# Rotary embedding of the first stage: from a rotation matmul on TensorE to a lane shuffle on VectorE, with a new order of work

## What is computed

```python
x = x + attn(layernorm(x))            # stage 0: the only one with the rotation
x = x + xattn(layernorm(x), ctx)      # stage 1
x = x + ffn(layernorm(x))             # stages 2 to 7, then a last layer norm

def _apply_rope(x, cos, sin):         # on queries and keys of stage 0, per head of 16 channels
    x1, x2 = (x[..., :8], x[..., 8:])
    return concatenate([x1 * cos - x2 * sin, x2 * cos + x1 * sin], axis=-1)
```

## Time and profile before

| | us |
|---|---|
| median of 3 runs | 5278.08 |
| lowest, highest | 5269.10, 5292.41 |
| the profiled execution: time | 5268.01 |
| the profiled execution: span | 5266.2 |
| PE busy in the span | 4823.1 |
| DVE busy | 3453.1 |
| ACT busy | 2479.3 |
| POOL busy | 707.9 |

### The profile page before, as it was taken

How to read it: one execution, slowest core, us unless ns; L and a number is a source line. 1 busy time by engine, 2 the same in 40 slices (tenths; PEclk the granted TensorE clock), 3 DMA queues, 4 the chain that set the end, 5 groups by cost and what they waited for, 6 DMA issues and landing times.

```text
span 5266.2 us, 149908 instructions
## 1 busy us (share of the span) xinstructions
PE 4823.1 (92%) x59612; PEld 3530.9 (67%) x59612; DVE 3453.1 (66%) x6058; ACT 2479.3 (47%) x4737; POOL 707.9 (13%) x1734
## 2 busy tenths in 40 slices
...
PEclk8999999999999999998999999999999999999999
...
DMA packets 42888, 44.64 MB, mean 8 GB/s; under 512 B 11552, under 2 KB 41888, under 8 KB 42144
## 3 DMA queue, kind: packets, MB, share of 16 engines
...
## 4 chain that ended last, share of the span: by engine, by line
issue 55%; PE 28%; DVE 7%; POOL 6%; ACT 1%; POOLq 1%; DVEq 0%; ACTq 0%
PE banks L945 27%; DVE row_max L909 3%; POOL neg_max L719 2%; POOL neg_max L722 2%; POOL x_tok L704 1%; POOL inv_std L698 1%; PE banks L1064 1%; DVE pair_sums L930 1%; ACT probs L818 1%; DVE rope_s L874 1%; DVE k_parts L887 0%; POOL var_eps L695 0%; PE banks L994 0%; DVE n_tok L930 0%; DVE x_tok L942 0%
## 5 line engine op out<-in xcount | busy, mean ns | idle before, releaser
L909 DVE TENSOR_REDUCE row_max<-banks 128x4 f32<-128x1024 f32 (+1 forms) x1280 | 1313.3, 1068 | 350.5 <-PE banks L945 348.0
L818 ACT ACTIVATE probs<-banks 128x1024 f32<-128x1024 f32 (+1 forms) x1280 | 1137.8, 935 | 487.6 <-PE banks L945 469.9
L945 PE MATMUL banks<-k_parts,q_parts 32*128 32x256 f32 (+1 forms) x15360 | 652.1, 306 | 166.8 <-DVE row_max L909 130.9
L945 PEld LDWEIGHTS banks<-k_parts,q_parts 32*128 32x128 f32 x15360 | 541.9, 201 | 333.7 <-DVE row_max L909 162.4
L930 DVE TENSOR_TENSOR pair_sums<-probs 128x512 f32<-128x512 f32 x512 | 368.1, 719 | 524.3 <-ACT probs L818 403.3
L945 PE MATMUL banks<-q_parts,k_parts 32*128 32x256 f32 (+1 forms) x13824 | 605.4, 304 | 75.1 <-DVE row_max L909 32.0
L945 PEld LDWEIGHTS banks<-q_parts,k_parts 32*128 32x128 f32 (+1 forms) x13824 | 470.6, 188 | 291.6 <-issue 163.4
L719 POOL TENSOR_TENSOR neg_max<-row_max,zeros 128x8 fp32r<-128x8 f32 x640 | 166.4, 260 | 3680.1 <-DVE row_max L909 3680.1
L945 PE MATMUL banks<-node_t,w_n 128*128 128x256 f32 x2560 | 633.2, 390 | 5.5 <-ACT node_t L835 5.5
L930 DVE TENSOR_TENSOR n_tok<-probs 128x512 f32<-128x512 f32 x512 | 364.2, 711 | 286.7 <-PE banks L945 167.9
L945 PEld LDWEIGHTS banks<-node_t,w_n 128*128 128x128 f32 x2560 | 461.4, 190 | 125.2 <-issue 46.1
...
## 6 DMA issues: line engine op xcount, KB each, us to landing
...
```

What stands on the lines that cost most here:

```text
L818: done(act.activation(probs[s][0:rows, g % 2, 2 * p:2 * p + 2, 0:kt, :] .rearrange("p c k t -> p c (k t)"), psum[0:rows, b0:b0 + 2, 0:kt * T],
L909: done(dve.reduce_max(row_max[s][:, g, 2 * p:2 * p + 2, :].rearrange("p c q -> p (c q)"), psum[:, b0:b0 + 2, :].rearrange("p c (q t) -> p ...
L945: return nc.tensor.matmul(bank_ap, lhs, rhs, start=start, stop=stop, **kw)
```

## The change

The matmul by rot is gone, for queries and keys (QR and KR, with their two banks). In its place DVE shuffles the lanes within each group of 32 partitions: lane p takes lane 16*(p//16) + (p+8)%16, which swaps the halves of each head. The sign goes into the sine table, once in the prologue: PE multiplies rot by a column of ones, and DVE multiplies the table by the resulting column. A copy of one element stands ahead of each shuffle. KI now waits for the shuffle of the queries and no longer for QR. The multiplication by the sines reads rope_s in SBUF, where it read a bank. And the whole ORDER is another one, with other banks; its new words are shown in parts.

```diff
+TURNED = [16 * (p // 16) + (p + 8) % 16 for p in range(ROWS)]
...
             elif k in ("QS", "KS"):
-                dve.wait_ge(sem["proj_ready"], reached(at, "proj_ready", (k[0] + "R", s, j)))
-
+                dve.wait_ge(sem["rope_in_kept"], reached(at, "rope_in_kept", (k[0] + "I", s, j)))
                 old = [("KH", 1 - s, j), ("KL", 1 - s, j)] if k == "QS" else [("QH", s, j, 1), ("QL", s, j, 1)]
                 dve.wait_ge(sem["high_kept"], reached(at, "high_kept", old[0]))
                 dve.wait_ge(sem["low_kept"], reached(at, "low_kept", old[1]))
-                done(dve.tensor_tensor(rope_s[:, :, :], both_of((k[0] + "R", s, j)),
+                dve.tensor_copy(rope_seen[:, :], rope_in[s][:, 0, 0:1])
+                done(dve.stream_shuffle(rope_s[:, :, :], halves(rope_in[s]), TURNED), "rope_turned", a)
+                dve.wait_ge(sem["rope_turned"], reached(at, "rope_turned", a))
+                done(dve.tensor_tensor(rope_s[:, :, :], rope_s[:, :, :],
                                        sin_t[:, :].unsqueeze(1).to_broadcast([P, KC, T]), ALU.mult), "rope_sin", a)
...
                 if k == "KI":
                     act.wait_ge(sem["rope_cos"], reached(at, "rope_cos", ("QC", s, j)))
-                    act.wait_ge(sem["proj_ready"], reached(at, "proj_ready", ("QR", s, j)))
+                    act.wait_ge(sem["rope_turned"], reached(at, "rope_turned", ("QS", s, j)))
...
-            elif k in ("QR", "KR"):
-                wait_for(pe, at, a, ("rope_in_kept", (k[0] + "I", s, j)))
-                done(matmul(bank_of(a), rot[:, :], rope_in[s][:, :, :].rearrange("p k t -> p (k t)"), True, True),
-                     "proj_ready", a)
...
+                pe.wait_ge(rest_loaded, 16 * len(rest_copies))
+                last = nc.tensor.matmul(psum[:, 0, NODES * KC:NODES * KC + 1], rot[:, :], all_ones[:, 0:1],
+                                        start=True, stop=True)
...
+                dve.tensor_scalar(sin_t[:, :], sin_t[:, :], psum[:, 0, NODES * KC:NODES * KC + 1], None,
+                                  ALU.mult).then_inc(chain_v, 1)
```

The order at the places that the prediction speaks of, old and new. The head of the table, that is the restart of the loop:

```diff
-KI0.1 LNP0.1 V1.0@5 LNN0.1 KS1.0 TR0.1@3 KH0.1 KL0.1 TRE0.1 KH1.0 KL1.0 Q0.1@6 QB0.1 QH0.1.0 QH0.1.1 QL0.1.1
-QL0.1.0 VE1.0 S1.0.0@0 SB1.0.0 MX1.0.0.0 MX1.0.0.1 S1.0.1@4 SB1.0.1 MX1.0.1.0 MX1.0.1.1 S1.0.2@0 SB1.0.2
+LOADX0 +LOADC0 LNP0.1 LNN0.1 VE1.0 KS1.0 KH0.1 TR0.1@0 TRE0.1 Q0.1@2 KL0.1 KH1.0 QB0.1 KL1.0 QH0.1.0 QH0.1.1
+QL0.1.1 S1.0.0@4 QL0.1.0 SB1.0.0 S1.0.1@0 MX1.0.0.0 SB1.0.1 MX1.0.1.1 MX1.0.0.1 MX1.0.1.0 S1.0.2@4 SB1.0.2
```

Stage 0 of slot 0, with the last stage of slot 1 (all words from the first projection to the first transposed scores):

```diff
-+Q0.0@2 +QB0.0 OB0.7.1 +QI0.0 FA0 S1.7.1@4 SB1.7.1
-MX1.7.1.0 +QR0.0@3 MT1.7.0@0 MR1.7.0 +QC0.0 +K0.0@2 +KI0.0 MX1.7.1.1 ST1.7.0@4 +QS0.0 +QH0.0.1 SX1.7.0 EX1.7.0.1
-EX1.7.0.0 NM1.7.1 MT1.7.1@0 MR1.7.1 LNS0.7 +QL0.0.1 +KR0.0@1 +KC0.0 +KS0.0 V1.7@2 VE1.7 +KH0.0 LNP0.7 ST1.7.1@4
-SX1.7.1 EX1.7.1.1 PV1.7.0@1 PA1.7.0.1 PA1.7.0.0 LNN0.7 PS1.7.0 RC1.7.0 +KL0.0 FG0 NR1.7.0 FX0 +V0.0@0 EX1.7.1.0
-+VE0.0 +S0.0.0@4 +SB0.0.0 +MX0.0.0.0 +MX0.0.0.1 +S0.0.1@0 +SB0.0.1 +MX0.0.1.0 +MX0.0.1.1 +NM0.0.1 PA1.7.1.1
-STORE0 +XB0.0 +LOADX1 OA1.7@5 +S0.0.2@0 +SB0.0.2 +MX0.0.2.1 +MX0.0.2.0 +NM0.0.0 PA1.7.1.0 PV1.7.1@4 +S0.0.3@0
-+SB0.0.3 +MX0.0.3.1 +MX0.0.3.0 OB1.7.0 +MT0.0.0@7 PS1.7.1 RC1.7.1 +MR0.0.0 +NM0.0.2 NR1.7.1 +NM0.0.3 +ST0.0.0@0
++Q0.0@5 MX1.7.0.0 +QB0.0 MX1.7.0.1 OB0.7.1 +QI0.0 FA0 S1.7.1@0 +QC0.0 SB1.7.1 NM1.7.0 MX1.7.1.0 MT1.7.0@5
+MR1.7.0 ST1.7.0@4 MX1.7.1.1 SX1.7.0 EX1.7.0.1 +QS0.0 +K0.0@3 EX1.7.0.0 V1.7@2 PA1.7.0.0 +KI0.0 NM1.7.1 PA1.7.0.1
++QH0.0.1 +KC0.0 +QL0.0.1 MT1.7.1@1 MR1.7.1 ST1.7.1@4 +KS0.0 VE1.7 SX1.7.1 EX1.7.1.1 PV1.7.0@1 PS1.7.0 LNS0.7
++KH0.0 LNP0.7 EX1.7.1.0 +KL0.0 RC1.7.0 PA1.7.1.0 +S0.0.0@4 +SB0.0.0 NR1.7.0 +V0.0@0 +MX0.0.0.0 +VE0.0 +MX0.0.0.1
+LNN0.7 +S0.0.1@4 +SB0.0.1 +NM0.0.0 FG0 +MX0.0.1.0 OA1.7@3 +MX0.0.1.1 +NM0.0.1 +S0.0.2@4 FX0 +SB0.0.2 STORE0
++MX0.0.2.0 PV1.7.1@1 +MX0.0.2.1 +XB0.0 PA1.7.1.1 +S0.0.3@4 +SB0.0.3 +MX0.0.3.1 +MT0.0.0@0 +LOADX1 +MR0.0.0
+PS1.7.1 RC1.7.1 OB1.7.0 +MX0.0.3.0 NR1.7.1 +ST0.0.0@4
```

The tail of the table, stage 0 of slot 1 ahead of the restart:

```diff
-+PV0.0.3 +PA0.0.3.1 +PA0.0.3.0 +PS0.0.3 +RC0.0.1 FX1 +QS1.0 STORE1 +NR0.0.1 +K1.0@1 +OB0.0.0@6 +OB0.0.1 +KI1.0
-+V0.1@1 +XA0.0 +LNS0.1 +VE0.1 +KC1.0 +QH1.0.1 +QL1.0.1 +KR1.0@6 +K0.1@2 +XB1.0
++QS1.0 +PS0.0.3 +XB1.0 +RC0.0.1 +OB0.0.0@0 +K1.0@2 +NR0.0.1 +OB0.0.1 +KI1.0 +V0.1@1 +QH1.0.1 +XA0.0 +KC1.0
++K0.1@6 +LNS0.1 +V1.0@3 +KI0.1 +VE0.1 +QL1.0.1
```

And two places in the later stages (the words of PE alone), transposed scores of stage 2 and of stage 4:

```diff
-V0.2@0 MT0.2.0@3 ST0.2.0@0
+MT0.2.0@7 V0.2@4 ST0.2.0@4
...
-MT0.4.1@3 S1.4.0@4 SB1.4.0 PV0.4.0@3 PS0.4.0 ST0.4.1@4
+S1.4.0@0 SB1.4.0 MT0.4.1@5 PV0.4.0@6 PS0.4.0 ST0.4.1@0
```

More of the change, by code:

```diff
@@ new lines @@
+MT0.1.1@2 ST1.0.2@4 PA1.0.1.0 SX1.0.2 EX1.0.2.1 PV1.0.1 PS1.0.1 EX1.0.2.0 PA1.0.2.1 MT0.1.0@1 RC1.0.0 PA1.0.2.0
+ST1.0.3@4 SX1.0.3 MR0.1.0 K1.1@3 EX1.0.3.0 PV1.0.2@1 EX1.0.3.1 PS1.0.2 MR0.1.1 PA1.0.3.0 ST0.1.0@4 SX0.1.0
+PA1.0.3.1 EX0.1.0.1 PV1.0.3 NR1.0.0 EX0.1.0.0 PS1.0.3 RC1.0.1 ST0.1.1@4 SX0.1.1 OB1.0.0@0 EX0.1.1.0 NR1.0.1
+V1.1@2 OB1.0.1 VE1.1 +LOADC1 KI1.1 XA1.0 PV0.1.0@1 EX0.1.1.1 PS0.1.0 LNS1.1 ST0.1.2@4 SX0.1.2 EX0.1.2.0 PV0.1.1
+LNP1.1 PS0.1.1 EX0.1.2.1 XB0.1 RC0.1.0 LNN1.1 ST0.1.3@4 SX0.1.3 EX0.1.3.0 NR0.1.0 TR1.1@3 EX0.1.3.1 PV0.1.2@2
@@ new lines @@
+SX1.1.2 K0.2@6 EX1.1.2.1 NR1.1.0 EX1.1.2.0 QH0.2.1 KH0.2 ST1.1.3@0 SX1.1.3 OB1.1.0@5 EX1.1.3.1 KL0.2 EX1.1.3.0
+QL0.2.1 PV1.1.2@4 QL0.2.0 S0.2.0@0 SB0.2.0 MX0.2.0.0 PS1.1.2 PV1.1.3 PS1.1.3 MX0.2.0.1 RC1.1.1 K0.3@6 NM0.2.0
+NR1.1.1 KH0.3 OB1.1.1 KL0.3 XA1.1 S0.2.1@0 SB0.2.1 LNS1.2 MT0.2.0@7 V0.2@4 MR0.2.0 MX0.2.1.1 LNP1.2 VE0.2
+MX0.2.1.0 ST0.2.0@4 LNN1.2 SX0.2.0 NM0.2.1 TR1.2@2 MT0.2.1@1 TRE1.2 MR0.2.1 K1.2@0 EX0.2.0.1 EX0.2.0.0 Q1.2@2
+KH1.2 PA0.2.0.0 QB1.2 PA0.2.0.1 QH1.2.0 PV0.2.0@3 KL1.2 QH1.2.1 PS0.2.0 QL1.2.0 RC0.2.0 S1.2.0@4 SB1.2.0
@@ new lines @@
+PS1.2.1 MX0.3.0.1 RC1.2.1 OB1.2.0 K1.4@1 NR1.2.1 MX0.3.0.0 OB1.2.1 KH1.4 NM0.3.0 NE1.2.0 S0.3.1@4 NE1.2.1
+SB0.3.1 MX0.3.1.0 MT0.3.0@0 Q1.3@3 MR0.3.0 QB1.3 MX0.3.1.1 V1.3@2 QH1.3.0 QH1.3.1 QL1.3.1 KL1.4 VE1.3 ST0.3.0@4
+QL1.3.0 SX0.3.0 NM0.3.1 S1.3.0@0 EX0.3.0.0 SB1.3.0 MX1.3.0.0 EX0.3.0.1 MX1.3.0.1 PV0.3.0@5 NM1.3.0 MT0.3.1@7
+PA0.3.0.1 MT1.3.0@4 MR0.3.1 ST0.3.1@0 PA0.3.0.0 SX0.3.1 EX0.3.1.0 PS0.3.0 K0.5@6 EX0.3.1.1 PA0.3.1.0 MR1.3.0
+PA0.3.1.1 RC0.3.0 S1.3.1@0 SB1.3.1 KH0.5 MX1.3.1.0 PV0.3.1@4 PS0.3.1 MX1.3.1.1 RC0.3.1 OA0.3@7 NR0.3.0 ST1.3.0@0
```

124 lines of the change are left out of this document (55 added, 69 removed).

## The result

The changed kernel takes 5462.3 us (median of 4 runs, 5437.8 to 5482.3), the kernel before on the same chip 5276.7: a ratio of 1.035, 95% interval 1.0315 to 1.0385. It is 3.5% slower. I had predicted 5244 us and a range of 5185 to 5325; the time lies outside the range, on the other side of "no change". Behind two of the later tables stand positions that I worked out from the traces: each step of the written order was found in the record of VectorE or ScalarE, its distance taken from LNN0.1, the first VectorE instruction of its turn, and the mean taken over the 15 turns of the loop.

A forecast was written before the change was run, and what follows sets the result against it. PE, 92% busy, looked like the bound, but DVE sets the pace during the row maxima. Terms +1.7 - 1.15 - 1.75 - 0.9 = -2.1 us a turn, times 16 is -34 us, giving 5244 us; range 5185 to 5325.

The forecast's parts named there:

- slot 0, QS0.0 to PA0.0.0.0: Slot 0's first stage: DVE is the limit and PE's saving is worth nothing; +1.7 us a turn.
- slot 1, up to the restart: Slot 1's first stage: PE loses 1.99 us, the query's 0.84 on DVE is charged in full; -1.15 us a turn.
- restart to MX1.0.0.0: Loop restart: value projection moved ahead, restart to slot 1's first scores falls from 7.70 to 5.96 us; -1.75 us a turn.
- the other stages: Remaining stages: new order mostly repeats the old with other bank numbers, two waits change; -0.9 us a turn, bounds +2 to -3.
- The shuffle's price: On DVE, each product costs one shuffle pass of 0.69 us and a one-element copy of 0.15, 0.84 us more.
- rival 4: On DVE, the shuffle takes 1.4 us or masks cost extra: 45 us more, 5289 us; chance 0.05.
- rival 2: Sine pass on DVE collides with POOL, up to 2.7 us a turn eat the gain: about 5278 us; chance 0.17.
- My bound of +2: Upper bound in us a turn for the other stages, for new waits that were not found.
- the 0.5 for the waits between query and key: Slot 0, ahead of the maxima: estimated us for waits for ScalarE that the new order puts between query and key.
- The group cycle: Slot 0's four score groups share one set of banks, so each takes a cycle of 3.44 us.
- 1.0 us comes back: Slot 0: keys' low parts no longer collide with POOL's gain and shift, 2.42 us for two instructions against 1.41.
- Rival 3: Clock falls each turn behind slot 0's maxima, costing 51 to 90 us: 5295 to 5334 us; chance 0.20.

The follow-up runs named there:

- e1: The changed kernel's shuffle and signed sines in the old order of work with its old banks, against the kernel before; 5305.2 us, ratio 1.0069.
- e10: e5 with slot 0's keys and their copy back in the old sequence, from the previous turn's last maxima to slot 0's value projection; 5409.5 us, ratio 1.0259.
- e8: e1 without copy and shuffle, so no engine does the rotation and VectorE multiplies unrotated queries and keys by the sines; 5254.8 us, ratio 0.9954.
- e5: Changed kernel with two transposes of slot 1's maxima moved behind slot 0's scores, and one maxima reduction moved later; 5415.3 us, ratio 1.0254.
- e9: e5 with the stretch from slot 1's first stage to the start of its second put back into the old sequence; 5365.0 us, ratio 1.0182.
- e16: e9 with one word moved: the variance of slot 0's next layer norm goes ahead of slot 0's bias sum on POOL; 5346.7 us, ratio 1.0137.
- e15: e1 with the new order in the later stages only, and the two transposes and the reduction moved as in e5; 5301.3 us, ratio 1.0051.

## Why the prediction was wrong

Its terms by the positions, us a turn:

| stretch | predicted | before | after | difference | e1 |
|---|---|---|---|---|---|
| slot 0, QS0.0 to PA0.0.0.0 | +1.7 | 27.40 | 30.24 | +2.8 | +1.5 |
| slot 1, up to the restart | -1.15 | 22.09 | 23.74 | +1.65 | +0.8 |
| restart to MX1.0.0.0 | -1.75 | 7.63 | 7.32 | -0.3 | -0.2 |
| the other stages | -0.9 | 264.77 | 271.49 | +6.7 | +0.4 |

The sum is +10.9 us a turn instead of -2.1; times 16 it is 175 us, and the profiled executions differ by 170.

- **The shuffle's price was right.** 0.730 and 0.146 us, 0.88 for the 0.84 of the forecast; rival 4 fell. The estimate by the Trainium skill, "VectorE: DVE Perf Modes", section on the perf-mode tiers, was 0.60; the measurement decides for one full pass. The mask load in front of it takes 13 ns. The sine pass, 697 ns in the mean, didn't become the collision of rival 2.
- **The step that failed most is "The other stages", -0.9 us.** "In most places the new order repeats the old with other bank numbers" is false for words that matter. I compared the sequences by their waits in the trace of before, which shows only what waited in the old order. Words moved ahead of something ready, on a queue in order, have no row there: MT1.3.0 and MT1.6.0 on PE (47 us), TR1.1 ahead of PV0.1.2 (50 with its neighbours, mostly through the clock), XB0.1 and LNP0.0 on POOL (18). My bound of +2 was set without a reason. The prediction named its own test, a move of over 2 us in the later stages means a reading too coarse; it was 6.7, of which 4.8 lie from LNS0.2 on.
- **Slot 0, +1.7, was under-sized by 1.1, ahead of the maxima.** From QS0.0 to the first maximum the mean grew from 11.25 to 12.93 us, +1.7 for the forecast's 0.5. The mis-sized term is the 0.5 for the waits between query and key: KS0.0 starts 6.10 us behind QS0.0, not 3.69, which is 1.5 more than the shuffle and its copy (0.9); the old sequence in e10 has it at 4.37. From the first maximum to PA0.0.0.0 it is +1.2, as forecast (12.7 - 11.55). The group cycle is right: 3.45 us between the pairs from the second on (767.38 to 770.83 to 774.28), for 3.44. The first cycle takes 3.90, as V0.0, which "lies in these gaps and costs nothing", ran at half clock for 3.29 us. And "1.0 us comes back" from the collision on the keys' low parts came (983 to 750 ns, 15 us in all), but the passes just named took more in other places: the apply 15.0, the rotated sum 14.4, the low queries 6.9 and the last x 16.5 us, 53 together. I counted the meeting that the change ends and none that it begins.
- **Slot 1 up to the restart, -1.15, had the wrong sign.** PE's 1.99 us were charged as a gain where PE waited anyway: e8 shows two thirds of the matmuls' time hidden, e1 shows DVE's passes in full. In the old order (e1) the stretch grew by 0.8; what the new order adds to it, another 0.9, no run took apart.
- **The restart, -1.75, was read from an untypical turn.** My 5.96 us from restart to first scores was exact: 809.87 - 803.84 = 6.03. But the 7.70 us that it replaced belong to a turn in which the value projection ran at half clock. In the timeline of the kernel before, turns 1 and 4 differ in just that:

```profile
460.31 1.99 PE L945 MATMUL banks<-w_qkv,h_t 128*128 128x256 f32 x8 [2.61 <-issue]
...
1428.01 3.56 PE L945 MATMUL banks<-w_qkv,h_t 128*128 128x256 f32 x8 [2.48 <-issue]
```

  Five of 15 turns (2, 4, 7, 8 and 12) have the half-clock stretch there; the mean to the first maximum was 7.6, not the 8.7 of my turn. The gain is 0.3.
- **Rival 3 was the nearest, with its mechanism in another place.** A new stretch at half clock is there in slot 0, but at the start of the maxima, behind PE's 3.93 us of waiting for the keys, not behind them; and it isn't alone. Its price, 51 to 90 us, was that of the clock in the end (82, below); its 5295 to 5334 us fell short by 130, since it had the clock as the only loss.

How much is the clock and how much is waiting can be told from the profiled executions, one of each kernel. A span is PE's idle time and its busy time, and half of what PE is busy in stretches at half clock is what the clock cost (an estimate: the value projection takes 1.99 us at the full clock and up to 3.56 in such a stretch), in us:

| profiled execution | span | PE idle | cost of the clock | the rest |
|---|---|---|---|---|
| before | 5266 | 443 | 167 | 4656 |
| changed | 5436 | 593 | 249 | 4594 |
| e5 | 5415 | 553 | 266 | 4597 |
| e9 | 5360 | 550 | 203 | 4606 |
| e16 | 5343 | 522 | 230 | 4591 |
| e15 | 5302 | 526 | 166 | 4611 |
| e1 | 5304 | 522 | 179 | 4604 |

The rest is 4591 to 4613 us in all sixteen kernels without the matmuls and 4650 to 4656 in the three with them, so the split holds to some 15 us. Of the 170 us between before and changed, waiting is +150, the clock +82 and the matmuls -62. The steps differ in kind: e5 is waiting (-40, with the clock at +17; it shows as 21 us here, since the profiled execution of the changed kernel was the fastest of its four), e9 is the clock (-62, with the waiting the same), e16 is waiting (-28, of which the clock takes 26 back), and from e16 to e15 it is the clock again (-64). No run changed the clock alone, so why it falls in one place and not in another stays open.
